# Two gated blocks on one core: batch 0 routed during the attention, batch 1's logits from raw rows, biases and rotations later

## What is computed

```
xn = layernorm(x)
QKV = xn @ W_in.T + b_in;  Q, K, V = split(QKV)
Q, K = rope(Q), rope(K)                       # first 128 features, interleaved pairs
A = sum over tokens of (K / |K|) * V          # one row per batch
s = (A * Q) @ W_out.T + b_out + xn
route = sigmoid(xn @ router_w);  e = argmax(route)      # 8 experts, one per token
h = silu(xn @ gate_w[e]) * (xn @ up_w[e])
g = silu((h @ down_w[e]) * max(route))
x = x + s * g
```

## Time and profile before

| | us |
|---|---|
| median of 3 runs (351.94 to 356.08) | 352.62 |
| the profiled run's own time | 353.23 |
| its span, first to last instruction | 351.2 |
| TensorE busy | 319.4 |
| VectorE busy | 230.7 |
| GpSimd busy | 67.4 |

### The profile page before, as it was taken

One profiled execution on the slowest core, in us unless ns is written; L12 is line 12 of the kernel. 1 busy time (PEld: TensorE's weight loads), 2 busy tenths in 40 slices (PEclk: granted clock), 3 DMA queues, 4 the chain that ended last, 5 costly groups with the idle time before them and its releaser, 6 DMA issues.

```text
span 351.2 us, 4689 instructions
## 1 busy us (share of the span) xinstructions
PE 319.4 (91%) x1598; PEld 188.7 (54%) x1598; DVE 230.7 (66%) x489; ACT 155.8 (44%) x282; POOL 67.4 (19%) x72
## 2 busy tenths in 40 slices
PE   3977799999999999999999999998986999999960
PEld 3655565445555544555554555465654566666640
DVE  3997849767575677877957711289995754456631
ACT  1477414676667455553674564411204222323220
POOL 4008650000020000000000000020673000346641
PEclk9999989999999999999999999998998999999997
DMA  7980000000000000000000040059226990424510
GB/s 245 411 218 2 0 1 2 0 4 0 1 3 2 1 0 3 0 0 4 1 2 1 0 167 15 0 216 367 77 97 189 400 424 32 154 89 136 154 51 11
DMA packets 11370, 30.56 MB, mean 87 GB/s; under 512 B 1773, under 2 KB 8014, under 8 KB 10064
## 3 DMA queue, kind: packets, MB, share of 16 engines
q1 hardware_dynamic: 9392, 26.01, 20.4%
q0 software_dynamic: 1952, 4.22, 3.9%
HBM read 27.22 MB, written 6.60 MB: 96 GB/s over the span
## 4 chain that ended last, share of the span: by engine, by line
PE 74%; DVE 14%; issue 3%; DMA 3%; POOL 2%; ACT 2%; DVEq 0%; POOLq 0%
PE ps L1578 11%; PE ps L1523 9%; PE ps L1491 8%; PE ps L1591 8%; PE ps L1513 7%; PE ps L1646 6%; PE ps L1632 5%; PE ps L1654 5%; PE ps L1428 3%; DVE nmax L1103 3%; PE ps L1453 2%; POOL slot_rows L787 2%; PE ps L1407 2%; PE ps L1622 1%; DMA x<-in_x 1%
## 5 line engine op out<-in xcount | busy, mean ns | idle before, releaser
L1103 DVE TENSOR_REDUCE nmax<-ps 128x1 f32<-128x512 f32 x128 | 85.5, 687 | 34.5 <-PE ps L1491 33.8
L907 ACT ACTIVATE shared<-ps 128x512 f32<-128x512 f32 x128 | 74.2, 594 | 53.8 <-PE ps L1513 52.7
L1491 PE MATMUL ps<-experts 96*128 96x512 bf16 x128 | 48.2, 384 | 1.6 <-DVE experts L1110 1.1
L1513 PE MATMUL ps<-experts 99*128 99x512 bf16 x128 | 48.5, 382 | 0.0
L1591 PE MATMUL ps<-shared,experts 128*128 128x256 f32 x128 | 38.0, 386 | 0.0
L1523 PE MATMUL ps<-shared,experts 128*32 128x512 f32 x256 | 34.1, 605 | 0.3 <-ACT shared L907 0.3
L1491 PEld LDWEIGHTS ps<-experts 96*128 96x128 bf16 x128 | 12.5, 98 | 36.7 <-DVE nmax L1103 18.3
L1591 PEld LDWEIGHTS ps<-shared,experts 128*128 128x128 f32 x128 | 23.3, 191 | 9.8 <-issue 3.4
L777 POOL TENSOR_TENSOR experts<-experts,late_weights 128x768 f32<-128x768 f32 x1 | 1.8, 1805 | 130.8 <-ACT experts L897 130.8
L1428 PE MATMUL ps<-late_weights,xnT 128*128 128x512 f32 (+1 forms) x64 | 23.9, 522 | 0.5 <-DVE shared L1069 0.5
L915 ACT ACTIVATE experts<-ps 96x1024 bf16<-96x1024 bf16 x18 | 17.9, 1018 | 11.6 <-PE ps L1453 11.6
(11 more groups left out here) (209 smaller groups left out, 526.9 us busy)
## 6 DMA issues: line engine op xcount, KB each, us to landing
experts<-in_experts SPq DMA_DIRECT2D x8, 1536.0 KB, 12.6
shared<-in_wgu SPq DMA_DIRECT2D x1, 2048.0 KB, 11.1
slot_rows<-in_empty SPq DMA_DIRECT2D x1, 1950.0 KB, 19.5
late_weights<-slot_rows SPq DMA_DIRECT2D x9, 130.0 KB, 4.2
x<-in_x SPq DMA_DIRECT2D x2, 512.0 KB, 5.5
shared<-in_wdn SPq DMA_DIRECT2D x1, 1024.0 KB, 13.1
token_rows<-x SPq DMA_DIRECT2D x1, 1024.0 KB, 14.4
token_rows<-gx SPq DMA_DIRECT2D x1, 1024.0 KB, 4.9
```

The costliest lines, as they stand in the source:

```text
L907: nc.scalar.activation(probs[:, n % 2, hh, :], ps[:, 2 + hh % 2, :], ACT.Exp, scale=float(HD) ** -0.5).then_inc(s["exp_done"], 1)
L1103: nc.vector.tensor_reduce(nmax[:, 4 * t + hh:4 * t + hh + 1], ps[:, m % 2, :], AX, ALU.max, negate=True).then_inc(s["max_done"], 1)
L1491: nc.tensor.matmul(ps[:, m % 2, :], qs[0:KS, b, GR * g + hh, P * t:P * t + P], ks[0:KS, b, g, :], start=True, stop=True).then_inc(s["score ...
L1513: nc.tensor.matmul(ps[:, 2 + hh % 2, :], ks[0:KM, b, g, P * t:P * t + P], qs[0:KM, b, GR * g + hh, :], start=True, stop=True).then_inc(s[" ...
```

## The change

- Batch 0 is routed by itself, in the attention's plan: one-hot and running sums (`route`) at steps 26 and 27, counts and slots at step 28. Its four indirect stores follow then. For that each expert has a fixed region of 1024 slots in `slot_rows` (8192 instead of 1920 rows to be emptied, in four transfers behind the row moves of units 0 to 3), and batch 1's rows go behind those of batch 0 in each region. SP reads the first row of an expert tile from `tile_r` before it loads it.
- Batch 1's logits are products of the raw rows x (transposed by TensorE, `raw_T`) with a router whose column means are taken off (`router_c`), scaled by the norm's inverse root afterwards. The norm itself runs beside them. ScalarE normalises two of the four row tiles.
- QKV tiles 1 to 3 are evacuated by ScalarE without bias; VectorE adds it to the three later in one operation, after the routing. The rotations, the products of key and value (before on GpSimd) and the key norms come later; two q transposes, both token sums and all branch products stand within the expert tiles, some between gate and up product (`PE_BETWEEN`, `DVE_BETWEEN`). All QKV tiles of TensorE stand ahead of the first expert tile.
- Eight results are held instead of seven, their finals come in tiles 7, 8 and 9 instead of 5 to 8, there are eleven slot-row buffers instead of eight, and the twelve filling transposes are gone.

The diff, cut to its core:

```diff
-SLOTS = MT * P
+REGION = TOK
+SLOTS = E * REGION
...
-XR = TOK // P
+XR = 11
...
+EMPTYINGS = 4
...
-HELD = SURE - 1
+HELD = SURE
...
+                           (26, 3, ("route", 0, 0)), (27, 1, ("route", 0, 1)), (27, 3, ("route", 0, 2)), (28, 1, ("counts", 0)),
+                           (28, 1, ("place", 0))):
...
-           *[("norm_root", last, stage) for stage in range(4)], ("norm_apply", last), *qkv1[3:],
-           ("rows_T", last, 0), ("rows_T", last, 1), ("rope1", 0), ("logits", last)]
+           ("qkv1_out", 0), ("wo", last, 0), ("norm_sums", last, 0), ("wo", last, 1), ("norm_sums", last, 1), qkv1[3], ("raw_T", 0),
+           *qkv1[4:6], ("raw_T", 1), ("qkv1_out", 1), qkv1[6], ("raw_logits",), *[("norm_root", last, stage) for stage in range(4)],
+           ("norm_apply", last), *qkv1[7:9], ("qkv1_out", 2), qkv1[9], ("rows_T", last, 0), ("rows_T", last, 1)]
...
-def side_work(i):
-    return {0: [("norm", 1)], 1: [("sum", 1)], 2: [("branch", 2)], 3: [("branch", 3)]}.get(i, [])
+PE_BETWEEN = {2: [("q_T", 3)], 3: [("branch", 0)], 4: [("sum", 1)], 5: [("branch", 3)]}
+PE_AFTER = {1: [("q_T", 2)], 2: [("sum", 0)], 3: [("branch", 1)], 4: [("branch", 2)]}
+DVE_BETWEEN = {1: [("sum_tiles", 0)], 3: [("branch", 0)], 4: [("sum", 1)], 5: [("branch", 3)]}
+DVE_AFTER = {0: [("rope", 1), ("product", 1)], 2: [("sum", 0), ("sum_tiles", 1)], 3: [("branch", 1)], 4: [("branch", 2)]}
+ACT_AFTER = {0: [("squares", 0)], 1: [("q_T", 2), ("squares", 1)]}
+FINALS = {SURE - 1: (0, 1, 2), SURE: (3, 4, 5), SURE + 1: (6, 7)}
+FINALS_LEFT = {SURE: (3, 4, 5, 6, 7), SURE + 1: (6, 7)}
...
+            if a < 8:
+                return late[:, (a - 3) * RW + lo:(a - 3) * RW + hi]
+            return Sa[:, 9216 + (a - 8) * RW + lo:9216 + (a - 8) * RW + hi]
...
-            sp.dma_start(xs_dram.rearrange("(i p) d -> p i d", p=P),
-                         empty_in.rearrange("p (o d) -> p o d", o=1).to_broadcast([P, MT, RW])).then_inc(s["slots_emptied"], 16)
...
+                if u < EMPTYINGS:
+                    sp.dma_start(blocks[:, some * u:some * u + some, :],
+                                 empty_in.rearrange("p (o d) -> p o d", o=1).to_broadcast([P, some, RW])).then_inc(s["slots_emptied"], 16)
...
-                sp.dma_start(slot_row(i), xs_dram[P * i:P * i + P, :]).then_inc(x_sem[i % XR], 16)
+                row = sp.value_load(tile_r[0:1, i:i + 1], min_val=0, max_val=SLOTS - P)
+                sp.dma_start(slot_row(i), xs_dram[bass.ds(row, P), :]).then_inc(x_sem[i % XR], 16)
...
+                    sp.wait_ge(s["tile_experts"], 1)
                     sp.wait_ge(s["scattered"], 16 * NT)
-                    sp.wait_ge(s["qkv1_psum"], NT)
                     for i in range(XR):
+                        if i == 3:
+                            sp.wait_ge(s["qkv1_psum"], NT)
                         load_rows(i)
-                    for a in range(FIRST_EXPERTS):
-                        expert_here(a)
+                        if i == 0:
+                            for a in range(FIRST_EXPERTS):
+                                expert_here(a)
...
-            def key_times_value(b):
-                pool.wait_ge(s["rope_q"], b + 1)
-                nc.gpsimd.tensor_tensor(kv[:, TB * b:TB * b + TB, :], qkv1[b][:, :, D:2 * D], qkv1[b][:, :, 2 * D:3 * D], ALU.mult
-                                        ).then_inc(s["kv_ready"], 1)
...
+            pool.wait_ge(s["router_mean"], 1)
+            nc.gpsimd.tensor_tensor(router_c[:], router[:], small[:, 1, 0:E].rearrange("p (o e) -> p o e", o=1).to_broadcast([P, KD, E]),
+                                    ALU.subtract).then_inc(s["router_centred"], 1)
...
+            def scatter(b):
+                pool.wait_ge(s["slots"], b + 1)
+                pool.wait_ge(s["slots_emptied"], 16 * EMPTYINGS)
+                pool.wait_ge(s["rows_norm"], NT + TB * (b + 1))
+                for j in range(TB * b, TB * b + TB):
+                    nc.gpsimd.indirect_dma_start(
+                        out=xs_dram[:, :], out_offset=bass.IndirectOffsetOnAxis(ap=smi[:, j:j + 1], axis=0),
+                        in_=xn[:, j, :], in_offset=None).then_inc(s["scattered"], 16)
+            scatter(0)
+            scatter(1)
             key_norms(0, pool, nc.gpsimd, chain)
             pool.sem_inc(s["norm_ready"], 1)
...
                 elif kind == "norm_apply" and it[1] < B - 1:
-                    apply_norm(it[1])
+                    act.wait_ge(s["up_ready"], NI)
...
+            qkv1_out(3)
+            xsT_copy(0)
+            for n in range(KD):
                 q_copy(n)
-            xsT_copy(0)
-            key_squares(1)
             for i in range(SURE):
...
+            def route(b, stage):
...
+                desc = const("desc").rearrange("p (o e) -> p o e", o=1).to_broadcast([P, TB, E])
+                if stage == 0:
+                    if b == 0:
+                        dve.wait_ge(*place(("logits", b))[1:])
+                    else:
+                        dve.wait_ge(s["gates_ready"], 1)
+                    chain(nc.vector.tensor_scalar_add(lg, lg, 1.0))
+                    chain(nc.vector.reciprocal(lg, lg))
+                    chain(nc.vector.tensor_reduce(prob, l3, AX, ALU.max))
+                    chain(nc.vector.tensor_tensor(l3, l3, prob.to_broadcast([P, TB, E]), ALU.is_ge))
+                elif stage == 1:
+                    nc.vector.tensor_scalar_mul(prob, prob, 0.25)
...
+                    chain(nc.vector.tensor_reduce(best, l3, AX, ALU.max))
+                    if b == 0:
+                        dve.wait_ge(s["ranks_clear"], 1)
...
+                    chain(nc.vector.tensor_tensor(earlier(1), earlier(0), earlier(0, 1), ALU.add))
+                    nc.vector.tensor_tensor(earlier(2), earlier(1), earlier(1, 2), ALU.add).then_inc(s["onehot"], 1)
...
+            def place_rows(b, bank, read):
...
+                dve.wait_ge(s["counts"], b + 1)
...
+                start = (region1 if b else const("region")).rearrange("p (o e) -> p o e", o=1).to_broadcast([P, TB, E])
+                chain(nc.vector.tensor_tensor(l3, bank[:, 0:TB * E].rearrange("p (j e) -> p j e", j=TB), start, ALU.add))
+                chain(nc.vector.tensor_tensor(l3, l3, onehot.rearrange("p (j e) -> p j e", j=TB), ALU.mult))
+                chain(nc.vector.tensor_reduce(at8.rearrange("p (j o) -> p j o", o=1), l3, AX, ALU.add))
+                nc.vector.tensor_copy(smi[:, TB * b:TB * b + TB], at8).then_inc(s["slots"], 1)
+                if b == 0:
+                    nc.vector.tensor_copy(small[:, 2, 0:E], bank[:, TB * E:PAIRS]).then_inc(s["tot0"], 1)
+                    dve.wait_ge(s["tot0"], 1)
+                    nc.vector.tensor_tensor(region1, small[:, 2, 0:E], const("region"), ALU.add).then_inc(read, 1)
...
+            dve.wait_ge(s["qkv1_copied"], TB - 1)
+            nc.vector.tensor_tensor(qkv1[0][:, 1:TB, :], qkv1[0][:, 1:TB, :],
+                                    bin_b.rearrange("p (o n) -> p o n", o=1).to_broadcast([P, TB - 1, 3 * D]), ALU.add).then_inc(s["bias_added"], 1)
+            qkv1_bias(TB)
             qkv1_bias(TB + 1)
+            rope1(0, 0)
             qkv1_bias(TB + 2)
-            dve.wait_ge(s["norm_ready"], 1)
-            sum_tiles(0)
+            rope1(0, 1)
             qkv1_bias(TB + 3)
-            scaled_output(0)
-            rope1(1)
-            branch(0)
-            branch(1)
...
-            finals = {SURE - 3: (0, 1), SURE - 2: (2, 3), SURE - 1: (4, 5), SURE: (6,)}
+            def last_rows(i, finals):
+                if i > SURE:
+                    for k in finals:
+                        final(k)
+                if i:
+                    result(i - 1)
+                if i <= SURE:
+                    for k in finals:
...
+            def counts(b, bank):
+                pe.wait_ge(s["onehot"], b + 1)
+                nc.tensor.matmul(bank[:, 0:PAIRS], const("ones"), earlier(2), start=True, stop=False)
+                nc.tensor.matmul(bank[:, 0:TB * E], const("before"), onehot, start=False, stop=True).then_inc(s["counts"], 1)
...
-            whole_qkv(TB)
-            whole_qkv(TB + 1)
-            pe.wait_ge(s["onehot"], 1)
-            nc.tensor.matmul(ps[:, 5, 0:NT * E + E], const("before"), onehot, start=True, stop=False)
-            nc.tensor.matmul(ps[:, 5, 0:NT * E + E], const("ones"), before_tile(3), start=False, stop=True).then_inc(s["counts"], 1)
-            whole_qkv(TB + 2)
+            counts(B - 1, ps[:, 5, :])
+            qkv(TB - 1, 1)
+            qkv(TB - 1, 2)
+            for j in range(TB, NT):
+                whole_qkv(j)
...
+                if i == 0:
+                    rows_T(1)
+                    pe.wait_ge(*qkv1_evacuated(NT - 1))
+                side_work(PE_BETWEEN.get(i, ()))
...
+            pe.wait_ge(s["tile_experts"], 1)
+            rows_T(0)
             q_T(0)
             q_T(1)
-            whole_qkv(TB + 3)
-            token_sum(0)
```

(13 more changed lines are left out.)

350 lines of the change are left out of this document (206 added, 144 removed).

## The result

The changed kernel takes 354.63 us (median of 12 runs, 352.25 to 358.15) against 352.46 for the kernel before (12 runs beside them): ratio 1.0055, 95% interval 1.0028 to 1.0082. It is 0.5% slower, 2.2 us by the medians. Forecast were 349.8 us and a range up to 354.0. The ratios leave out runs in a slower state, over 1.5% above the fastest of the same kernel; the medians hold all runs. The profiled run has a span of 352.3 us (own time 354.38).

What follows compares the result with a forecast made beforehand. TensorE's work bounds the attention and tiles, its waits on routing and slot rows the stretch between, a dependent chain the end. 353.23 + 1.0 - 7.5 + 3.7 gives 350.4, forecast 349.8 us because that run is 0.6 over the median; range 344.0 to 354.0.

Steps and rivals of the forecast that it cites:

- The attention, + 1.0: In the attention: 8 added narrow passes on full TensorE cost 1.0 us (0 to 1.6).
- The emptying at nothing: In the attention: emptying 8.5 MB of slots instead of 2.0, behind the row moves of units 0 to 3, costs 0.
- 225.3 to tile 0, 13.2 us less: Between attention and expert tiles: tile 0 starts at 256.8, 13.2 us ahead of 270.04.
- the wait for the bias: Before tile 0: TensorE waits 1.45 us for batch 1's QKV bias, which VectorE does late, to 249.8.
- The tiles, 67.0: Tile 0 to tile 10: 61.2 us plus 4.8 moved work, minus 0.7, plus 1.7 waits; tile 10 starts at 323.8.
- Rival 3: Clock falls from narrow products and waits around the first tiles: one gives 351.5, two 353.2; chance 0.09.
- At the end, 3.7 given back: In the tail: result 8 waits for its gather, so the last hidden transposes start at 335.6, not 331.9 (3.1 to 5.9).
- Only the branch (2.18 us of issue) held TensorE up.: Last hidden transposes, kernel before: their rows were ready in time, and only 2.18 us of branch issue delayed them.
- The last pieces, 6.17 from the transposes to the last store: After the last hidden transposes: part of the closing dependent chain, which the change leaves alone.
- tile 0 after 261: Sign of error at the first tile: VectorE's queue is longer than summed.
- the attention over 2 us longer: Sign of error: the attention ends over 2 us later, by the shared bank or the emptying.
- GpSimd at rest in the tail: Sign of error in the tail: GpSimd was forecast busy without rest from 315 to 341.

Runs made afterwards that it cites:

- g1: Kernel before, its eleven tiles written out on TensorE without reading the number of tiles and without a branch: 351.34 us, ratio 0.9964.
- k1: Kernel before with the repaired kernel's edits to the tail (finals' order, no spare gathers, result 9 before tile 10's down product): 353.92 us, ratio 1.0023.
- e3: Changed kernel with three eighths of the slot emptying, in three transfers instead of four: 355.41 us, ratio 1.0039.
- repaired kernel: Changed kernel with earlier finals, result 8's first step ahead and rest deferred, later tanh, no spare gathers, result 9 before tile 10's down product: 346.99 us, ratio 0.9808.
- h2: Repaired kernel with twelve filling transposes behind tile 9's down product and six ahead of tile 10's: 347.81 us, ratio 0.9844.
- f1: Changed kernel with result 8's first step ahead of final results 6 and 7 in tile 9: 354.56 us, ratio 1.0066.
- e1: Changed kernel with 22 filling transposes ahead of tile 9's hidden transposes and 30 ahead of its down product: 354.73 us, ratio 1.0041.
- e4: Changed kernel with final results 4 and 5 moved from tile 8 into tile 9: 355.13 us, ratio 1.0051.
- k2: Changed kernel with only the two gathers for absent tiles 11 and 12 left out: 354.93 us, ratio 1.0040.

## Why the prediction was wrong

The direction was wrong, and the time by 4.8 us. In front of the end the sum held; the end had a wait that the sum took at nothing. Step by step:

- **The attention, + 1.0.** Right. The first QKV of layer 1 starts at 224.86 against 225.33, but the kernel before was profiled with a fall of the clock at 45 to 49 us and the changed one without. Of the profiles of the changed kernel and its variants, five with this fall alone have tile 0 at 257.6 to 258.1, six without one at 256.0 to 256.5, so it is worth about 1.5 us. The kernel before without the fall (g1, k1) has the first QKV at 223.67 and 223.89, so the attention has grown by 1.0 to 1.2. The emptying at nothing fits as well, as far as e3 can tell.
- **225.3 to tile 0, 13.2 us less.** Right: 31.3 us from the first QKV to tile 0, forecast 31.5, before 44.5. The first store started at 242.10 (I had 243.05), the wait for the bias was 0.35.
- **The tiles, 67.0.** Nearly right, 67.66, but the waits were shared out otherwise. Behind ScalarE's squares and the tanh of tile 2 TensorE waited 0.65 us (1.1 forecast), for the q copy 1.74 (0.35 forecast), since VectorE had waited for the key norms. Rival 3, falls of the clock at these places, didn't occur: there is none from 228 to 330, though TensorE waited 1.41 us ahead of tile 0 and 1.74 in tile 2.
- **At the end, 3.7 given back. This step failed.** It is 8.5: from tile 10's gate product to the last store 22.84 us instead of 14.33. I had followed one wait to its end, the gather, result 8, tile 10's gated product, and had the hidden rows ready at 11.7 us after the gate product; they were ready at 13.0. That part had the right mechanism: the first store came 0.9 us later than forecast (315.43 against 314.5) and the gather of tile 8 1.6 later (330.79 against 329.2), its landing took 3.40 us (3.45 forecast). But I let TensorE wait for nothing else, and the transposes came 1.8 us after their rows were ready. The same final results stand ahead of result 8's *first* step, which releases the down bank and ScalarE's tanh, and behind that tanh stand tile 10's tanh and the hidden copy of tile 9. So tile 9's down product was late as well (+10.68 instead of +4.09).
- **"Only the branch (2.18 us of issue) held TensorE up."** I took these 2.18 us for something that ends with the other waits. They are part of 3 to 5 us that begin with the start of the down product (g1: 1.7 without the tests and the branch). Late product, late transposes: +14.80, where +11.8 was forecast.
- **The last pieces, 6.17 from the transposes to the last store, taken as unchanged.** They took 8.04. The clock was down: 0.46 more on the transposes, 1.40 on the product. That part of rival 3 came true at a place that I hadn't named. Held up in the repaired kernel (h2), it gave 0.7 us in a profile and nothing in the median, so the clock's share is 0 to 1.9 us, and it is the least certain piece here.

The account of the profiled spans: forecast 348.4; + 0.7 in the tiles, + 3.0 for the hidden transposes (1.2 for rows that were ready later, 1.8 for the late down product), + 1.9 behind them, - 1.5 for the fall at 45 us that this run didn't have, - 0.1 in front: 352.4, measured 352.3. What would show it wrong was named as tile 0 after 261, the attention over 2 us longer, or GpSimd at rest in the tail, and none of the three occurred: the list lacked ScalarE.

Three sums of the prediction are off by themselves, and none of them explains the miss. Its own range comes out at 348.2 to 352.6 from its terms, not 348.6 to 353.0. Its small operations put the slots at 242.4 and not 242.75 (the first store was at 242.10). A gather's landing of 2.6 us would have taken 0.85 us off the give-back and not 0.6; the landings here were 3.1 to 3.6 us.

What stays open: how often the falls of the clock at 45 and at 182 us occur in either kernel (by the start of tile 0 in the profiles they cost 1.5 and 1.7 us), and why f1's 1.2 us aren't in its median.

## What to carry to other kernels

Work that starts earlier is worth only what the end of the program lets through. When everything moves ahead except a slow stream at the end (here the indirect transfers of GpSimd, two a tile, 2.66 us), look at each instruction in the queues of *all* engines that stands behind an instruction waiting for that stream, its first small step above all, since that one frees a bank and another engine. Put steps that release others ahead of steps that wait, and issue nothing for tiles that don't exist. And what the trace shows as a loss need not cost: e1 took the low clock away, e4 a wait, k2 two spare gathers, and each won nothing, since the next in line was as late.

## What was unexpected of the hardware

- The branch to the drain on TensorE: where nothing else holds them, the next products start 3.1 to 4.9 us after the start of the 8 passes ahead (what spreads it isn't shown), 1.73 without a branch, 1.98 and 2.56 (0.68 of it a wait for VectorE) with the test turned round; the three branches to tiles 8 to 10 that this brings cost nothing visible (67.66 us for the tiles, as in the changed kernel). Whether the 8 passes run at 2.4 GHz (1.99 us, e1) or at 1.2 (3.78, the changed kernel) makes little difference: 4.44 and 4.12.
- Gathers of 128 rows landed 3.1 to 3.6 us after the start of their issue, as far as VectorE's waits show it (318 to 335 us in the changed kernel), when GpSimd issued without rest, and a row of gathers and stores ran at 1.33 us each, as before.
